# One column-tiled run per half batch for values and denominators, and head-by-head probability sums on GpSimd

## The chip, the core and the metric

One core of a Trainium2 chip runs the whole kernel. The metric is the device time of one execution in microseconds (us), median of the runs. Engines are named as in the profile: PE (TensorE matmul), PEld (its weight loads), ACT (ScalarE), DVE (VectorE), POOL (GpSimd), SP (the queue that issues most DMAs).

## The reference

Cross attention with low-rank corrections on every projection, 16 batches, 112 queries, 375 context rows, width 1024, 32 query heads on 8 key/value heads of size 32. The softmax is per query head; the output projection is added to the input.

```python
q = _lora_linear(hidden_states, Wq, Aq, Bq)   # (16, 112, 32 heads x 32)
k = _lora_linear(traces, Wk, Ak, Bk)          # (16, 375, 8 heads x 32)
v = _lora_linear(traces, Wv, Av, Bv)
scores = einsum('bhqd,bhtd->bhqt', q, k) / sqrt(32)
attn = softmax(scores, axis=-1)
context = einsum('bhqt,bhtd->bhqd', attn, v)
out = hidden_states + _lora_linear(context, Wo, Ao, Bo)
```

## The kernel before, in words

All of it runs in float32, as sums of three fast products (high and low parts). First the low-rank factors are folded into the weights and all queries are projected and written to memory (up to about 270 us of the span). Then comes a loop over the 16 batches, one step per batch of two halves; a half holds four key/value heads with four query heads each, so 448 columns per head group. After the loop the output projection runs over 14 row tiles (from about 930 us).

A step works on three batches at once, and its work is cut into pieces that `half_order` puts into one list per half. Every engine walks the same list in order and does its own share of each piece:

- **V** (values of the next batch, 3 PE matmuls of 256 columns, lines 803 to 807), **T** (transposes of the context of the batch after it; PE line 748, then ACT copies the high part, line 970, and DVE subtracts for the low part, line 1168), **K** (keys of that batch, 3 matmuls of 376 columns, lines 663 to 665). These three are the dense pieces. V is in half 0, K in half 1 (K0.k the first four heads, K1.k the second four), T in both.
- **S i**, i from 0 to 11: the scores of a head group and one of three context chunks (PE line 842, 448 columns), then `Exp` on ACT into `probs` (line 1037). S goes to bank `STB` or to bank `DEN`.
- **N i**, 0 to 15: a score matmul of the *next* batch for its row maxima (PE line 853), reduced by DVE (line 1246). N i waits until the maximum of N i-2 is taken. **M** turns the 16 maxima (PE line 858), ACT negates them (line 1044).
- **P c**, c from 0 to 2: the product of the probabilities of chunk c with the values, four matmuls that each write 32 of the 128 output columns of the array (column tiles), line 868. **D**: the denominators of the half *before*, four such matmuls on `prob_sum` with a matrix of ones (line 904), then ACT copies them (`copy_den`, line 1058) and SP stores them.
- **A**: DVE copies the attention output of the half before out of its bank (line 1228). **I, J**: DVE takes the reciprocal of the denominators, SP stores it.
- **E0 j, F0 j** and **E1 j, F1 j**: the keys leave their banks; E is two ACT copies of 32x376 (line 977), F one DVE subtraction (line 1173). E0/F0 are the first four heads, E1/F1 the second four.
- POOL adds the probabilities of the three chunks into `prob_sum` in two instructions of 1792 columns (lines 644 and 649).

The dense pieces stand in a fixed order; the others are placed by the table `PLAN` (kind, number, due time as a fraction of the half) among them, by counting the columns in `COST`. What is still in the table when the dense pieces are through is put behind them. `run_steps` says which kinds are in which step; steps 0 to 13 are full or nearly so, the last two also fold the output weights (**W**) and begin the output (**O**, **Z**). Engines and queues are in order, so a piece that waits holds all that is behind it on its engine.

## Time and profile before

| | |
|---|---|
| runs | 1071.17, 1073.62, 1074.78 us; median 1073.62 |
| span of the profiled execution | 1069.5 us (first to last instruction); the page gives no other time for it, and the median run is 4.1 us above it |
| PE busy | 997.3 us, 93% of the span |
| DVE, ACT, POOL busy | 582.0, 496.0, 286.3 us |
| granted PE clock, mean | 0.971 of full speed |
| one batch in the loop | 40.2 us (the first P of one half 0 at 512.66, of the next at 552.87) |

PE is busy nearly all the time, but a busy matmul row is not a matmul at its peak: rows overlap, so the distance from one row's start to the next one's start is what an instruction costs the engine. Idle time of DVE, ACT and POOL costs nothing unless PE waits for them.

### The profile page before, as it was taken

To read this page: it belongs to the slowest core of one execution; us is meant where nothing else is said; L and a number is where in the kernel's file an instruction comes from. 1 tells how busy PE (TensorE), PEld (TensorE's weight loads), DVE (VectorE), ACT (ScalarE), POOL (GpSimd) and SP (SyncE) were. 2 spreads that over 40 slices of the span, in tenths; PEclk is the share of its full clock that TensorE was granted. 3 is DMA by queue.
4 is the path that set the end of the run, shared out by engine and by line. 5 is a ranking of instruction groups with operands and counts; after the bars stand their busy time and mean duration, and the time that the engine had idled before them with its cause. 6 is when DMAs were issued, how large, how long until landed. Compare 5 with 4: busy or idle time off the path is not lost.

```text
span 1069.5 us, 17947 instructions
## 1 busy us (share of the span) xinstructions
PE 997.3 (93%) x5904; PEld 787.8 (74%) x5904; DVE 582.0 (54%) x1005; ACT 496.0 (46%) x971; POOL 286.3 (27%) x84
## 2 busy tenths in 40 slices
PE   6988899959999999999999999999999877999998
PEld 5878799958777777777777777777777533678886
DVE  5660213237766666666666666666666565233331
ACT  3340212234566666666666666666666544200100
POOL 1201000000344344344344344344344355300000
PEclk9999899979999999999999999999999959999999
DMA  6827342272223333333332332332331333567552
GB/s 189 233 78 200 126 149 77 78 179 76 66 94 99 68 93 96 67 93 92 71 93 91 73 93 88 75 93 87 77 93 38 84 112 84 142 206 235 183 170 78
DMA packets 104052, 118.13 MB, mean 110 GB/s; under 512 B 29152, under 2 KB 88672, under 8 KB 104016
## 3 DMA queue, kind: packets, MB, share of 16 engines
q1 hardware_dynamic: 100156, 103.99, 35.4%
q10 hardware_dynamic: 3860, 13.67, 3.5%
q8 instruction: 21, 0.34, 0.1%
q14 instruction: 15, 0.12, 0.0%
HBM read 87.59 MB, written 29.82 MB: 110 GB/s over the span
## 4 chain that ended last, share of the span: by engine, by line
PE 74%; DVE 7%; ACT 6%; DMA 6%; issue 4%; SPq 2%; ACTq 0%; POOL 0%; DVEq 0%; POOLq 0%
PE ps L663 11%; PE ps L664 11%; PE ps L665 11%; PE ps L853 9%; PE ps L868 8%; PE ps L842 7%; PE ps L748 4%; PE ps L803 3%; PE ps L805 3%; PE ps L807 3%; PE ps L904 3%; DMA ctx_in<-in_ctx_dram 2%; DMA q_scratch<-q_out_lo 2%; ACT probs L1037 2%; DMA out_dram<-residual 1%
## 5 line engine op out<-in xcount | busy, mean ns | idle before, releaser
L1246 DVE TENSOR_REDUCE maxima<-ps 112x1 f32<-112x375 f32 x512 | 271.0, 543 | 107.8 <-PE ps L853 101.1
L1037 ACT ACTIVATE probs<-ps 125x448 f32<-125x448 f32 x384 | 206.8, 543 | 132.8 <-PE ps L842 128.6
L644 POOL TENSOR_TENSOR prob_sum<-probs 125x1792 f32<-125x1792 f32 x32 | 129.2, 4039 | 391.8 <-ACT probs L1037 391.8
L853 PE MATMUL ps<-k_stack,q_stack 96*112 96x376 f32 x512 | 190.2, 372 | 7.0 <-DVE maxima L1246 5.5
L842 PE MATMUL ps<-q_stack,k_stack 97*125 97x448 f32 x384 | 147.9, 385 | 10.5 <-ACT probs L1037 10.2
L853 PEld LDWEIGHTS ps<-k_stack,q_stack 96*112 96x112 f32 x512 | 91.6, 179 | 85.8 <-DVE maxima L1246 69.0
L649 POOL TENSOR_TENSOR prob_sum<-prob_sum,probs 125x1792 f32<-125x1792 f32 x32 | 129.0, 4032 | 32.6 <-ACT probs L1037 32.5
L977 ACT ACTIVATE k_stack<-ps 32x376 fp32r<-32x376 f32 x256 | 121.4, 474 | 10.0 <-PE ps L665 6.1
L803 PE MATMUL ps<-wv_hi,ct_hi 128*125 128x256 f32 x384 | 112.6, 293 | 0.5 <-DVE k_stack L1173 0.5
L1168 DVE TENSOR_TENSOR ct_lo<-ps,ct_hi 128x375 fp32r<-128x375 f32 x128 | 70.2, 549 | 76.2 <-ACT ct_hi L970 75.6
L807 PE MATMUL ps<-wv_hi,ct_lo 128*125 128x256 f32 x384 | 108.4, 282 | 0.0
L805 PE MATMUL ps<-wv_lo,ct_hi 128*125 128x256 f32 x384 | 108.4, 282 | 0.0
L663 PE MATMUL ps<-xt_hi,wq_hi 128*128 128x448 f32 x256 | 98.7, 386 | 7.8 <-DVE q_out_lo L1162 7.1
L868 PE MATMUL ps<-probs,v 125*32 125x448 f32 x768 | 93.8, 560 | 7.6 <-ACT probs L1037 7.6
L970 ACT ACTIVATE ct_hi<-ps 128x375 fp32r<-128x375 f32 x128 | 61.9, 484 | 73.9 <-PE ps L748 71.9
L663 PE MATMUL ps<-wo_hi,attn_hi 128*128 128x512 f32 x224 | 89.9, 401 | 6.6 <-DVE attn_lo L1274 5.9
L664 PE MATMUL ps<-xt_lo,wq_hi 128*128 128x448 f32 x256 | 95.2, 372 | 0.0
L665 PE MATMUL ps<-xt_hi,wq_lo 128*128 128x448 f32 x256 | 95.0, 371 | 0.0
L1173 DVE TENSOR_TENSOR k_stack<-ps,k_stack 32x376 fp32r<-32x376 f32 x128 | 70.0, 546 | 37.7 <-ACT k_stack L977 35.0
L663 PE MATMUL ps<-ct_hi,wk_hi 128*128 128x376 f32 x256 | 89.5, 349 | 0.4 <-DVE ct_lo L1168 0.3
L664 PE MATMUL ps<-wo_lo,attn_hi 128*128 128x512 f32 x224 | 89.1, 398 | 0.0
L665 PE MATMUL ps<-wo_hi,attn_lo 128*128 128x512 f32 x224 | 89.1, 398 | 0.0
(80 smaller groups left out, 1465.4 us busy)
## 6 DMA issues: line engine op xcount, KB each, us to landing
ctx_in<-in_ctx_dram SPq DMA_DIRECT2D x16, 1500.0 KB
q_stack<-q_scratch SPq DMA_DIRECT2D x96, 224.0 KB, 4.3
x_in<-in_x_dram SPq DMA_DIRECT2D x8, 896.0 KB, 9.3
q_scratch<-q_out_hi SPq DMA_DIRECT2D x16, 448.0 KB, 2.8
q_scratch<-q_out_lo SPq DMA_DIRECT2D x16, 448.0 KB, 3.7
attn_scratch<-attn SPq DMA_DIRECT2D x32, 224.0 KB, 4.5
attn_rows<-attn_scratch SPq DMA_DIRECT2D x14, 512.0 KB, 4.9
inv_tile<-inv_scratch SPq DMA_DIRECT2D x56, 128.0 KB, 5.1
```

The source lines that it names most:

```text
L644: pool.tensor_tensor(prob_sum[:, :, :], probs[:, 0, :, :], probs[:, 1, :, :], ALU.add).then_inc(psum_added, 1)
L663: pe.matmul(dst, l_hi, r_hi, start=start, stop=False)
L664: pe.matmul(dst, l_hi, r_lo, start=False, stop=False)
L665: return pe.matmul(dst, l_lo, r_hi, start=False, stop=stop)
L803: pe.matmul(dst, ct_hi[:, k, rows], wv_hi[:, k, :], start=(k == 0 and i != 1), stop=False, skip_group_check=True)
L805: pe.matmul(dst, ct_hi[:, k, rows], wv_lo[:, k, :], start=False, stop=False, skip_group_check=True)
L807: mm = pe.matmul(dst, ct_lo[:, k, rows], wv_hi[:, k, :], start=False, stop=(k == KC - 1), skip_group_check=True)
L842: pe.matmul(ps[0:TR, score_bank(i), 0:QH], kst[cur][0:STM, g, c * TR:(c + 1) * TR], qst[cur][0:STM, g, :], start=True, stop=True).then_inc ...
L853: mm = pe.matmul(ps[0:NQ, NAT + i % 2, 0:NTE], qst[nxt][0:STK, g, rr * NQ:(rr + 1) * NQ], kst[nxt][0:STK, g, :], start=True, stop=True)
L868: mm = pe.matmul(ps[HD * j:HD * (j + 1), CTX, 0:QH], v_sb[cur][:, i, g * HD:(g + 1) * HD], probs[:, i, j, :], start=(i == 0), stop=(i == T ...
L1037: act.activation(probs[:, c, j, :], ps[0:TR, score_bank(i), 0:QH], ACT.Exp, scale=SM).then_inc(exp_done, 1)
L1246: dve.tensor_reduce(maxima[:, h, i:i + 1], ps[0:NQ, NAT + i % 2, 0:NT], AX.X, ALU.max).then_inc(max_done, 1)
```

## The change

In `PLAN` the three P pieces become one, due at 0.815 of the half, and its cost in `COST` rises from 4 to 16 times 448 columns; D has no cost any more and costs nothing on PE. Inside P, PE does the three value chunks (12 column-tiled matmuls) and at once the denominators of the *same* half (4 more). S is due every 0.065 instead of 0.07, N every 0.047 instead of 0.052, E0/F0 every 0.05 from 0.58 instead of every 0.08 from 0.62. E1/F1 move from the start of the next step's half 0 to the end of half 1, behind the last K. All odd S go to bank `DEN` and all even ones to `STB`, so S 1 now waits until ACT has copied the denominators of the half before (`den_copied`). POOL adds in eight instructions of 448 columns, one per head group, each behind its own `Exp`. SP's D waits for the earlier stores of denominators before it loads them back.

```diff
-S_IN_DEN = (3, 5, 7, 9, 11)
+S_IN_DEN = (1, 3, 5, 7, 9, 11)
 PLAN = sorted(
-    [("S", i, 0.01 + 0.07 * i) for i in range(TC * JH)]
-    + [("P", 0, 0.31), ("P", 1, 0.583), ("P", 2, 0.925), ("A", 0, 0.048), ("D", 0, 0.097)]
+    [("S", i, 0.01 + 0.065 * i) for i in range(TC * JH)]
+    + [("A", 0, 0.005), ("D", 0, 0.03), ("P", 0, 0.815)]
     + [("I", 0, 0.35), ("J", 0, 0.45)]
-    + [("N", i, 0.03 + 0.052 * i) for i in range(JH * RH)] + [("M", 0, 0.925)]
-    + [("E0", j, 0.62 + 0.08 * j) for j in range(JH)] + [("E1", j, 0.03 + 0.06 * j) for j in range(JH)]
-    + [("F0", j, 0.62 + 0.08 * j) for j in range(JH)] + [("F1", j, 0.03 + 0.06 * j) for j in range(JH)],
+    + [("N", i, 0.02 + 0.047 * i) for i in range(JH * RH)] + [("M", 0, 0.80)]
+    + [("E0", j, 0.58 + 0.05 * j) for j in range(JH)] + [("E1", j, 0.82 + 0.01 * j) for j in range(JH)]
+    + [("F0", j, 0.58 + 0.05 * j) for j in range(JH)] + [("F1", j, 0.82 + 0.01 * j) for j in range(JH)],
...
-COST = {"S": QH, "P": 4 * QH, "D": 4 * QH, "N": NTE, ...
+COST = {"S": QH, "P": 16 * QH, "N": NTE, ...
...
+        if piece[0] == "K" and piece[2] == KC - 1:
+            early = [item for item in order if item[0] in (f"E{piece[1]}", f"F{piece[1]}")]
+            order = [item for item in order if item not in early] + early
...
-                        if kind == "S" and i == 2 * JH - 1:
+                        if kind == "S" and JH <= i < 2 * JH:
+                            j = i - JH
+                            if j == 0:
+                                at_least(pool, den_done, n)
+                            pool.wait_ge(exp_done, NS * n + i + 1)
+                            pool.tensor_tensor(prob_sum[:, j, :], probs[:, 0, j, :], probs[:, 1, j, :], ALU.add
...
-                            pe.wait_ge(exp_done, NS * n + JH * (i + 1))
-                            if i == 0:
-                                at_least(pe, attn_set, n)
-                                pe.wait_ge(v_set, 2 * (b + 1))
-                            for j in range(JH):
...
-                            mm.then_inc(pv_done, 1)
-                        elif kind == "D":
-                            denominators(n - 1)
+                            pe.wait_ge(exp_done, NS * (n + 1))
+                            at_least(pe, attn_set, n)
+                            pe.wait_ge(v_set, 2 * (b + 1))
+                            for c in range(TC):
+                                for j in range(JH):
+                                    g = h * JH + j
+                                    mm = pe.matmul(ps[HD * j:HD * (j + 1), CTX, 0:QH],
+                                                   v_sb[cur][:, c, g * HD:(g + 1) * HD], probs[:, c, j, :],
+                                                   start=(c == 0), stop=(c == TC - 1))
+                                mm.then_inc(pv_done, 1)
+                            denominators(n)
...
-                            at_least(act, psum_added, 2 * n - (1 if c < 2 else 0))
+                            at_least(act, psum_added, SUMS * (n - 1) + j + 1 + (JH if c == 2 else 0))
```

With these numbers P's due time is reached only when the dense pieces are through, so P stands behind all of them. On PE, around the end of half 1 and the start of the next step (L663 to L665 keys, L868 values times probabilities, L858 maxima turned, L904 denominators, L803 to L807 next values, L842 scores), there stood before:

```order
L663 MATMUL ps<-ct_hi,wk_hi 128x376
L664 MATMUL ps<-ct_lo,wk_hi 128x376
L665 MATMUL ps<-ct_hi,wk_lo 128x376
L862 REGISTER_ALU
L868 MATMUL ps<-probs,v_81 32x448 x4
L857 REGISTER_ALU
L858 MATMUL ps<-ident,maxima 16x112
L803 MATMUL ps<-wv_hi,ct_hi 125x256
L805 MATMUL ps<-wv_lo,ct_hi 125x256
L807 MATMUL ps<-wv_hi,ct_lo 125x256
L829 REGISTER_ALU
```

and now (all lines are some ten higher: L673 to L675 keys, L878 values, L868 maxima, L913 denominators):

```order
L673 MATMUL ps<-ct_hi,wk_hi 128x376
L674 MATMUL ps<-ct_lo,wk_hi 128x376
L675 MATMUL ps<-ct_hi,wk_lo 128x376
L867 REGISTER_ALU
L868 MATMUL ps<-ident,maxima 16x112
L872 ISA
L878 MATMUL ps<-probs,v_81 32x448 x12
L911 REGISTER_ALU
L913 MATMUL ps<-prob_sum,ones 32x448 x4
L813 MATMUL ps<-wv_hi,ct_hi 125x256
```

M moved ahead of P, and the run of 16 column-tiled matmuls is the last work of the half.

On DVE, at the end of the same half (L1246 maxima, L1173 subtraction of the keys, L1228 copy of the attention output), there stood before, the loop's branch being the border of the step:

```order
L1173 TENSOR_TENSOR k_stack_78<-ps,k_stack_78 32x376
L1245 REGISTER_ALU
L1246 TENSOR_REDUCE maxima<-ps 112x1
L1245 REGISTER_ALU
L1246 TENSOR_REDUCE maxima<-ps 112x1
L1173 TENSOR_TENSOR k_stack_78<-ps,k_stack_78 32x376
L1245 REGISTER_ALU
L1246 TENSOR_REDUCE maxima<-ps 112x1
L1173 TENSOR_TENSOR k_stack_78<-ps,k_stack_78 32x376
```

and now (L1254 maxima, L1181 keys, L1236 attention copy):

```order
L1181 TENSOR_TENSOR k_stack_79<-ps,k_stack_79 32x376
L1253 REGISTER_ALU
L1254 TENSOR_REDUCE maxima<-ps 112x1
L1253 REGISTER_ALU
L1254 TENSOR_REDUCE maxima<-ps 112x1
L1181 TENSOR_TENSOR k_stack_79<-ps,k_stack_79 32x376
L1253 REGISTER_ALU
L1254 TENSOR_REDUCE maxima<-ps 112x1
L1181 TENSOR_TENSOR k_stack_79<-ps,k_stack_79 32x376 x5
L1234 REGISTER_ALU
L1236 COPY attn_66<-ps 128x448
```

The order of the first subtractions and maxima is the same; the four subtractions of the second heads now stand right behind the fourth one, ahead of the attention copy.

On ACT the same end of half 1 is, with the change (L1045 exponentials, L985 key copies, L1052 negated maxima, L1066 copied denominators; the branch is the border of the step):

```order
L1045 ACTIVATE probs<-ps 125x448
L985 ACTIVATE k_stack_78<-ps 32x376 x2
L1052 ACTIVATE neg_max<-ps 16x112
L982 REGISTER_ALU
L131 REGISTER_ALU
L985 ACTIVATE k_stack_78<-ps 32x376 x8
L394 REGISTER_ALU
L394 COMPARE_AND_BRANCH
L1045 ACTIVATE probs<-ps 125x448
L1066 ACTIVATE denominators<-ps 128x448
L1045 ACTIVATE probs<-ps 125x448 x5
```

The eight key copies stand in one block ahead of the next step's first exponential, and the copy of the denominators behind that exponential.

## Rows read from the trace of the kernel before

**Rows 1.** The page: busy time by engine; granted PE clock in 40 slices, in tenths.

```profile
PE 997.3 (93%) x5904; PEld 787.8 (74%) x5904; DVE 582.0 (54%) x1005; ACT 496.0 (46%) x971; POOL 286.3 (27%) x84
...
PEclk9999899979999999999999999999999959999999
```

**Rows 2.** Timeline of PE, 510 to 531 us: start, duration, line, operation, [idle before <-releaser].

```profile
511.22 0.36 PE L842 MATMUL ps<-q_stack,k_stack 97*125 97x448 f32 x1
511.69 0.43 PE L853 MATMUL ps<-k_stack,q_stack 96*112 96x376 f32 x1
512.66 0.96 PE L868 MATMUL ps<-probs,v 125*32 125x448 f32 x8 [0.54 <-ACT probs L1037]
...
517.60 0.36 PE L842 MATMUL ps<-q_stack,k_stack 97*125 97x448 f32 x1
517.89 0.96 PE L868 MATMUL ps<-probs,v 125*32 125x448 f32 x8
518.78 0.42 PE L853 MATMUL ps<-k_stack,q_stack 96*112 96x376 f32 x1
519.04 0.48 PE L748 MATMUL ps<-ident,ctx_in 125*128 125x125 f32 x3
...
525.61 0.48 PE L748 MATMUL ps<-ident,ctx_in 125*128 125x125 f32 x3
...
526.66 0.34 PE L853 MATMUL ps<-k_stack,q_stack 96*112 96x376 f32 x1
527.26 0.54 PE L748 MATMUL ps<-ident,ctx_in 125*128 125x125 f32 x3 [0.26 <-DVE ct_lo L1168]
```

**Rows 3.** Line 868 from 517.5 to 519: ns min/median/max, first and last start.

```profile
L868 PEld LDWEIGHTS ps<-probs,v x8: 105/108/109, 517.9 to 517.9; 125*32 125x32 f32 x8
L868 PE MATMUL ps<-probs,v x8: 538/551/564, 517.9 to 518.3; 125*32 125x448 f32 x8
```

**Rows 4.** Timeline of PE, 530 to 553 us.

```profile
539.06 0.34 PE L663 MATMUL ps<-ct_hi,wk_hi 128*128 128x376 f32 x1
...
539.58 0.33 PE L663 MATMUL ps<-ct_hi,wk_hi 128*128 128x376 f32 x1
...
540.10 0.34 PE L853 MATMUL ps<-k_stack,q_stack 96*112 96x376 f32 x1
540.28 0.37 PE L842 MATMUL ps<-q_stack,k_stack 97*125 97x448 f32 x1
540.49 0.33 PE L663 MATMUL ps<-ct_hi,wk_hi 128*128 128x376 f32 x1
```

**Rows 5.** Timeline of ACT, 536 to 553 us.

```profile
539.09 0.54 ACT L1037 ACTIVATE probs<-ps 125x448 f32<-125x448 f32 x1
539.66 0.96 ACT L977 ACTIVATE k_stack<-ps 32x376 fp32r<-32x376 f32 x2
540.69 0.54 ACT L1037 ACTIVATE probs<-ps 125x448 f32<-125x448 f32 x1
...
542.15 1.96 ACT L977 ACTIVATE k_stack<-ps 32x376 fp32r<-32x376 f32 x4
```

**Rows 6.** Timeline of DVE, 536 to 553 us.

```profile
539.46 0.54 DVE L1173 TENSOR_TENSOR k_stack<-ps,k_stack 32x376 fp32r<-32x376 f32 x1
540.03 0.55 DVE L1246 TENSOR_REDUCE maxima<-ps 112x1 f32<-112x375 f32 x1
540.65 0.54 DVE L1173 TENSOR_TENSOR k_stack<-ps,k_stack 32x376 fp32r<-32x376 f32 x1
```

**Rows 7.** Groups by line: busy us, mean ns of one | idle before.

```profile
L644 POOL TENSOR_TENSOR prob_sum<-probs 125x1792 f32<-125x1792 f32 x32 | 129.2, 4039 | 391.8 <-ACT probs L1037 391.8
...
L1058 ACT ACTIVATE denominators<-ps 128x448 f32<-128x448 f32 x32 | 17.4, 543 | 17.4 <-PE ps L904 17.1
```

**Rows 8.** Timeline of PE, 843 to 932 us.

```profile
850.56 0.74 PE L842 MATMUL ps<-q_stack,k_stack 97*125 97x448 f32 x1 [2.46 <-ACT probs L1037]
...
877.18 0.80 PE L663 MATMUL ps<-wo_hi,attn_hi 128*128 128x512 f32 x1 [3.68 <-DVE attn_lo L1274]
```

More of the change, by code:

```diff
@@ L42 @@
 NS = TC * JH
+SUMS = 2 * JH
 NN = JH * RH
@@ L112, in half_order @@
         at += COST[piece[0]]
+        if piece[0] == "K" and piece[2] == KC - 1:
+            early = [item for item in order if item[0] in (f"E{piece[1]}", f"F{piece[1]}")]
+            order = [item for item in order if item not in early] + early
     order += [(kind, i, 0) for kind, i, _ in plan]
-    assert "K" not in has or order.index(("K", 0, KC - 1)) < order.index(("E0", 0, 0))
+    for half in range(HALVES if "K" in has else 0):
+        assert order.index(("K", half, KC - 1)) < order.index((f"E{half}", 0, 0))
     return order + [("E", 0, 0)]
@@ L382, in run_steps @@
         def run_steps(eng, step, wo_factors):
-            full = ({"A", "D", "V", "T", "N", "Q", "E1"}, {"A", "D", "G", "T", "K", "C", "N", "Q"})
+            full = ({"A", "D", "V", "T", "N", "Q"}, {"A", "D", "G", "T", "K", "C", "N", "Q"})
             step(-1, 0, (set(), {"K"}))
-            step(-1, 1, ({"V", "T", "N", "E1"}, {"T", "K", "C", "N"}))
+            step(-1, 1, ({"V", "T", "N"}, {"T", "K", "C", "N"}))
             wo_factors()
@@ L391, in run_steps @@
             step(B // 2 - 2, 1, (full[0], full[1] - {"C"}))
-            step(B // 2 - 1, 0, ({"A", "D", "V", "N", "E1"}, {"A", "D", "G", "N", "W0"}))
+            step(B // 2 - 1, 0, ({"A", "D", "V", "N"}, {"A", "D", "G", "N", "W0"}))
             step(B // 2 - 1, 1, ({"A", "D", "W1"}, {"A", "D", "G", "W2"}))
@@ L567, in step @@
                         elif kind == "D":
+                            if "G" in has[h]:
+                                at_least(sp, den_stored, 16 * 2 * b)
                             store_den(sp, 2 * b + h - 1, b - 1 + h, 1 - h)
@@ L640, in step @@
                     for kind, i, k in half_order(h, has[h]):
[L641 to L649 removed]
+                        if kind == "S" and JH <= i < 2 * JH:
[4 more added lines that the diff above has]
+                            pool.tensor_tensor(prob_sum[:, j, :], probs[:, 0, j, :], probs[:, 1, j, :], ALU.add
+                                               ).then_inc(psum_added, 1)
+                        elif kind == "S" and i >= 2 * JH:
+                            j = i - 2 * JH
+                            pool.wait_ge(psum_added, SUMS * n + j + 1)
+                            pool.wait_ge(exp_done, NS * n + i + 1)
+                            pool.tensor_tensor(prob_sum[:, j, :], prob_sum[:, j, :], probs[:, 2, j, :], ALU.add
                                                ).then_inc(psum_added, 1)
@@ L900, in denominators @@
             def denominators(n):
-                pe.wait_ge(psum_added, 2 * n + 2)
+                pe.wait_ge(psum_added, SUMS * (n + 1))
                 for j in range(JH):
@@ L911, in _ @@
             run_steps(pe, step, wo_factors)
-            denominators(2 * B - 1)
             def tile(pair, par):
@@ L1029, in step @@
                         elif kind == "E1":
[L1030 removed]
+                            k_hi(b + 2, cur, 1, i)
                         elif kind == "S":
```

18 lines of the change are left out of this document (3 added, 15 removed).

## The prediction, made before the changed kernel ran

> **What bounds the kernel now.** I read the page first: PE is busy for 93% of the span and the granted clock is full in nearly every slice [rows 1], so a time is gained where PE's issue gets shorter or a wait of PE goes, and lost where PE waits anew. Then the timeline of PE inside one batch of the loop. Two things are to be seen there.
>
> First, a column-tiled run costs more than its streaming. A score matmul is followed by the next row after 0.21 us (540.28 to 540.49) [rows 4], but by P after 0.29 (517.60 to 517.89) [rows 2]; P takes 0.89 to the next row (517.89 to 518.78); and the row behind it takes 0.26 (518.78 to 519.04) where such a row takes 0.18 (540.10 to 540.28) [rows 4]. One run of four matmuls so costs 0.89 + 0.08 + 0.08 = 1.05 us. Inside it there are eight records in two passes of four, the second starting about 0.40 behind the first: 0.96 for all eight less 0.54 for the last, less the 0.02 by which the four of a pass are staggered [rows 2, 3]. The second pass needs no more than 0.40 either, so the rest of the 0.89 is 0.09 of emptying.
>
> Second, PE waits at three places of each batch, two in half 0 and one as half 1 begins: N 3 comes 0.47 behind S instead of 0.21 (511.22 to 511.69), the first P 0.97 behind N instead of 0.26 (511.69 to 512.66, for ACT's exponential), and T 5 comes 0.60 behind N instead of 0.18 (526.66 to 527.26, for DVE's low part) [rows 2]. That is 0.26 + 0.71 + 0.42 = 1.4 us of the 40.2 that a batch takes; without waits it would take 38.8.
>
> **The change, part by part, per batch.**
>
> *Merging.* Four runs per half become one of eight passes: 7 x 0.40 + 0.49 + 0.16 = 3.45 instead of 4 x 1.05 = 4.20, so 0.75 to 0.8 per half, **-1.6 us** per batch with the four entries and exits unrounded. No row shows two groups back to back. If nothing is gained between groups except the three entries and exits, it is 3 x 0.17 = 0.5 per half (-1.0); if passes follow each other without their 0.03 of slack, 0.95 per half (-1.9). I take 0.40, since a pass behind a pass is what the trace has. The trace shows all eight weight loads starting at 517.9, 0.4 us before the second pass that uses four of them [rows 3]. The Trainium skill ("TensorE: Matmul & The Clock Gate", Part 3, on what overlaps) says that a weight load overlaps matmuls in flight only if it is for other row groups; all of these use the same 125 rows, so by that rule each pass would show its load and merging would give only the entries and exits, -1.0 a batch, and the time of the third rival below. The trace here speaks against it.
>
> *Old waits.* P now stands behind all S, T 5 is separated from T 4 by the run, and half 0 has no E1/F1 in its ACT and DVE queues: **-1.4**.
>
> *New wait at S 1.* The odd banks are now shared with the denominators, and ACT copies these behind the first exponential, since it stands behind it in its queue. In half 1 the run's end is zero; K0.0 takes 0.52 + 0.09, so S 0 is issued at 0.6, its exponential starts 0.40 later (0.37 of matmul and 0.03), the copy follows some 0.5 behind and takes 0.54 [rows 4, 7]: done at 2.0. S 1 has only N 0, T 5 and N 1 ahead of it (0.18 + 0.33 + 0.25, T with its longer successor) and could go at 1.5. Wait 0.55. In half 0 ACT first finishes the eight copies of E1: they begin some 0.5 behind the start of the run and take 4 x 0.98 (1.96 for four) [rows 5], so they end about 1.2 us behind its end; exponential and copy end at 2.3, S 1 could go at 1.7. Wait 0.65. Together **+1.2**.
>
> *New wait at the end of half 1.* This is the largest. The order is S 8, N 11, K, first pair, N 12, S 9, K, second pair, N 13, K, S 10, N 14, third pair, K, N 15, S 11, fourth pair, K, K, M, P (with "pair" for the two E0 copies of one head and its F0). ACT can do an exponential and a pair every 1.60 us (539.09 to 540.69) [rows 5], and on DVE each F0 stands ahead of the next maximum: F starts 0.03 behind its pair (539.66 + 0.96 to 540.65), the maximum 0.57 behind F [rows 5, 6]. With the exponential of S 8 at zero, F 0 starts at 1.6, the maximum of N 12 ends at 2.7, that of N 13 at 4.3, that of N 15 at 6.0. PE, at 0.18 for N, 0.21 for S and 0.52 for K [rows 4], would be at N 14 at 2.3, and must wait for N 12's maximum: 0.4. It would then be at N 15 at 3.4, and waits for N 13's to 4.3: 0.9. It is at M at 5.75 and waits for N 15's to 6.0: 0.2. **+1.5.** Before, the same pairs stood 0.08 of a half apart, with more K between, and PE did not wait: K, K, N, S follow without a gap [rows 4].
>
> *New wait at the end of half 0.* N 15 now stands behind T 3 on DVE. A T needs 1.6 us from issue to the end of its low part (525.61 to 527.26, less 0.05) [rows 2], and the maximum behind it ends at 2.2; M is only 1.8 behind T 3. **+0.45.** The same chain delays N 12 and N 14 (behind T 1 and T 2) by 0.2 to 0.25 each, **+0.5**. In half 1, T 7's low part and then the reciprocal stand ahead of the maxima for N 8 and N 10: about **+0.6**.
>
> *E1/F1* then run beside the 3.3 us of the merged run, the fourth pair's tail excepted (counted at S 1). *POOL's* eight adds cost about 4039/4 = 1.0 us each [rows 7]; the last begins when the last exponential ends, before the run starts, and the denominators come 6 x 0.40 = 2.4 us into it: nothing. *SP's* extra wait is for a store of the half before: nothing. The DMAs of M, of the context and of the queries are needed half a step later or more: nothing, unless the half shrinks by several us.
>
> Sum per batch: -1.6 - 1.4 + 1.2 + 1.5 + 0.45 + 0.5 + 0.6 = **+1.2 us**. The single waits are good to 0.1 or 0.2 each, the sum to 0.8. Steps 0 to 13 make 14 x 1.2 = **+17**.
>
> *Ends.* In the last four halves merging gains about 1 us each, since some of it is at the low clock: -4. PE waits there 3.68 for the first tile of the output (877.18) [rows 8], because the fourth fold stood last in its half; it now stands in the middle: -3. In the step before the loop, four F1 in a row stand ahead of the first maxima: +2. Together **-5**, and the folds moved among the maxima could make it 0 or -12.
>
> So the profiled execution would have 1069.5 + 17 - 5 = 1081.5 of span; the median run lies 4.1 above the span, hence **1085.5 us**, 1.1% slower.
>
> **Rivals.**
>
> *Faster.* The new waits don't add up: where S 1 has waited, ACT and DVE are ahead, and less is left for the later places. The point from which it decides is their sum: below 3.0 us per batch (merging and the old waits) the change gains. If the end of half 1 and the T chains cost nothing, and only S 1 stays, a batch gains 1.8, 14 x 1.8 = 25, with the ends 1044 us. For it: nothing in the list except P forbids PE to run dense, and DVE and ACT are busy only 54 and 46%. Against: those are averages, and in the stretch of the pairs ACT is full [rows 5]. 0.20.
>
> *A wash.* New waits of 3.0 to 3.5 instead of 4.25: within 3 us of before, which is about what a measurement of this kernel can tell from no change (0.3%). 0.12.
>
> *The run doesn't merge,* each group empties the array before the next as it did alone. Then -1.0 instead of -1.6 per batch, 14 x 0.6 = 8 more: 1094. For it: no row of two groups in sequence. Against: the loads that start early [rows 3]. 0.10.
>
> *The clock.* It fell to 1.2 GHz in one slice late in the kernel [rows 1], where PE had idle gaps of 2.46 and 3.68 us [rows 8]. If the new waits let it fall in the loop, the merged run alone would cost 3.3 us more in a half: some 45 us in all over half of the halves, 1130. Against: none of the new waits is over 1 us, and the loop held 2.4 GHz with waits of 0.7. 0.03.
>
> **How the numbers follow.** The forecast has 0.55; with the two slower rivals slower has 0.68, same 0.12, faster 0.20. The forecast's own range is 14 x (0.4 to 2.0) with the ends at 0 to -12: 1073 to 1101. To hold 8 in 10 the range takes in the wash and the nearer part of the faster case and leaves out its far part and the clock: 1060 to 1101.
>
> **What would show it.** Right: P and D as one group of 32 records lasting 3.3 to 3.5 us; a batch of 41 to 42 us; PE waits for `maxima` and, at the second score matmul of each half, for the copied denominators; no wait of P for an exponential of more than 0.1. Wrong in the merging if the group takes 3.6 or more; wrong in the waits if a batch is under 40 us, or if the waits for `maxima` in the last 5 us of half 1 sum to under 0.7.

## The result, and the profile after

The changed kernel takes **1092.73 us** (median of 4 runs, 1091.31 to 1096.95) against 1072.55 (median of 4 runs): ratio 1.0203, 95% interval 1.0173 to 1.0233. It is 2% slower. Of all executions behind the times here and below one is left out of its ratio: 1351.61 us of a later kernel, at a mean granted clock of 0.655.

| | before | after |
|---|---|---|
| span of the profiled execution | 1069.5 us | 1090.4 us |
| first half step of the loop, step 0 | 21.20 us | 29.17 us |
| half 0 / half 1, mean of steps 1 to 13 | 21.03 / 19.17 us | 20.77 / 20.56 us |
| one batch | 40.20 us | 41.33 us |
| from the first S of step 14 to the last PE row | 238.3 us | 236.0 us |

A half is counted from the start of its S 0 on PE to the next half's S 0. The 20.9 us of span are: step 0 with +9.0 (half 0 +8.0, half 1 +1.0), 13 steps of +1.13 = +14.7, the rest of the kernel -2.3, and -0.45 at the loop's start.

From the page of after, the two lines that answer to [rows 1]:

```profile
PE 990.9 (91%) x5904; PEld 807.6 (74%) x5904; DVE 579.8 (53%) x1005; ACT 489.8 (45%) x971; POOL 320.6 (29%) x276
...
PEclk9999999989999999999999999999999957989999
```

PE is busy 6 us less in a span that is 21 us longer: the merging took work off PE, and new waits took more than that back.

The timeline of PE in one batch of the loop (half 1 ends with the run at 516.03), against [rows 2, 4]:

```profile
500.64 0.47 PE L852 MATMUL ps<-q_stack,k_stack 97*125 97x448 f32 x1 [0.57 <-ACT denominators L1066]
...
507.01 0.43 PE L863 MATMUL ps<-k_stack,q_stack 96*112 96x376 f32 x1 [0.28 <-DVE maxima L1254]
507.27 0.38 PE L852 MATMUL ps<-q_stack,k_stack 97*125 97x448 f32 x1
...
512.67 0.43 PE L863 MATMUL ps<-k_stack,q_stack 96*112 96x376 f32 x1 [0.22 <-DVE maxima L1254]
512.93 0.34 PE L673 MATMUL ps<-ct_hi,wk_hi 128*128 128x376 f32 x1
...
514.23 0.42 PE L863 MATMUL ps<-k_stack,q_stack 96*112 96x376 f32 x1 [0.61 <-DVE maxima L1254]
514.49 0.37 PE L852 MATMUL ps<-q_stack,k_stack 97*125 97x448 f32 x1
...
515.84 0.26 PE L868 MATMUL ps<-ident,maxima 112*16 112x112 f32 x1
516.03 2.46 PE L878 MATMUL ps<-probs,v 125*32 125x448 f32 x24
518.31 0.94 PE L913 MATMUL ps<-prob_sum,ones 125*32 125x448 f32 x8
519.18 0.38 PE L813 MATMUL ps<-wv_hi,ct_hi 128*125 128x256 f32 x1
...
521.65 0.47 PE L852 MATMUL ps<-q_stack,k_stack 97*125 97x448 f32 x1 [0.59 <-ACT denominators L1066]
```

The run is one group of 32 records, 3.15 us from 516.03 to 519.18. Around it PE waits at S 1 of both halves for the copied denominators and at N 8, N 14 and N 15 of half 1 for maxima; half 0, which follows, has two more, at N 14 (0.48 behind its predecessor, where 0.20 is usual) and at M (0.44, where 0.12 is usual):

```profile
532.84 0.36 PE L852 MATMUL ps<-q_stack,k_stack 97*125 97x448 f32 x1
533.32 0.43 PE L863 MATMUL ps<-k_stack,q_stack 96*112 96x376 f32 x1
...
536.05 0.26 PE L868 MATMUL ps<-ident,maxima 112*16 112x112 f32 x1 [0.16 <-DVE maxima L1254]
```

The idle time in brackets understates a wait: by distances between starts, N 15 comes 0.95 behind its predecessor where 0.17 is usual. The view of waits sums them up:

```profile
PE ps L863 <- DVE maxima L1254: 28.1, 46, 7.7
...
PE ps L852 <- ACT denominators L1066: 20.3, 30, 2.7
```

What they wait for is seen on the other two engines in the same stretch. ACT, against [rows 5], does the eight E1 copies, then the exponential of S 0, then the denominators, which end as S 1 of half 0 starts:

```profile
516.69 3.91 ACT L985 ACTIVATE k_stack<-ps 32x376 fp32r<-32x376 f32 x8
520.62 0.54 ACT L1045 ACTIVATE probs<-ps 125x448 f32<-125x448 f32 x1
521.06 0.54 ACT L1066 ACTIVATE denominators<-ps 128x448 f32<-128x448 f32 x1
```

DVE, against [rows 6], does each F0 ahead of the maximum that PE needs:

```profile
513.05 0.54 DVE L1181 TENSOR_TENSOR k_stack<-ps,k_stack 32x376 fp32r<-32x376 f32 x1 [0.43 <-ACT k_stack L985]
513.62 1.00 DVE L1254 TENSOR_REDUCE maxima<-ps 112x1 f32<-112x375 f32 x2
514.66 0.55 DVE L1181 TENSOR_TENSOR k_stack<-ps,k_stack 32x376 fp32r<-32x376 f32 x1
```

At the two ends of the loop two places stand out. In step 0, PE has the longest idle time of steps 0 to 13, and its clock falls: the granted clock from 271 to 277 us is 0.50, the 1.2 GHz level, where the kernel before has 1.00 from 268 to 280 us.

```profile
271.34 0.74 PE L852 MATMUL ps<-q_stack,k_stack 97*125 97x448 f32 x1 [6.36 <-DVE a_stack_o L1131]
```

```profile
core 0: us, PE busy (x) PEld busy (x) DVE busy (x) ACT busy (x) POOL busy (x), PEclk, DMA share, GB/s
271.00:277.00 6.00, 5.66 (x23) 5.50 (x24) 2.39 (x5) 1.40 (x3) 0.00 (x0) 0.50 0.01 3
```

DVE of the changed kernel there, and of the kernel before:

```profile
266.50 0.55 DVE L1181 TENSOR_TENSOR k_stack<-ps,k_stack 32x376 fp32r<-32x376 f32 x1 [0.44 <-ACT k_stack L985]
267.58 2.45 DVE L1126 TENSOR_TENSOR b_stack_o<-b_in,b_stack_o 32x1024 fp32r<-32x1024 f32 x2 [0.53 <-ACT b_stack_o L951]
270.06 1.23 DVE L1131 SCALAR_TENSOR_TENSOR a_stack_o<-ps,a_stack_o 64x1024 fp32r<-64x1024 f32 x1
```

```profile
263.70 2.45 DVE L1118 TENSOR_TENSOR b_stack_o<-b_in,b_stack_o 32x1024 fp32r<-32x1024 f32 x2 [1.22 <-ACT b_stack_o L943]
266.18 1.23 DVE L1123 SCALAR_TENSOR_TENSOR a_stack_o<-ps,a_stack_o 64x1024 fp32r<-64x1024 f32 x1
```

The factor's low part comes 3.9 us later, behind the F1 block of the step before, and S 1 is now the first score in the bank that the factor's transposes used.

In step 14, half 1 takes 32.0 us instead of 25.4, with a new wait of PE of 7.73 us for maxima at 889.76; on DVE the normalising and splitting of the first output tile stand ahead of these:

```profile
889.76 0.66 PE L863 MATMUL ps<-k_stack,q_stack 96*112 96x376 f32 x1 [7.73 <-DVE maxima L1254]
```

```profile
883.55 3.35 DVE L1277 TENSOR_TENSOR attn_rows<-attn_rows,inv_tile 128x1024 f32<-128x1024 f32 x1
888.03 1.22 DVE L1282 TENSOR_TENSOR attn_lo<-attn_rows,attn_hi 128x1024 fp32r<-128x1024 f32 x1 [1.12 <-ACT attn_hi L1072]
889.17 0.99 DVE L1254 TENSOR_REDUCE maxima<-ps 112x1 f32<-112x375 f32 x2
```

### The profile page after: what moved, and what is told of

Its sections match the earlier page's. It is cut to its first block and busy times, and to the rows that moved or that the text cites. A ratio compares the mean times of both kernels' runs of the same rounds, so it can differ in the third digit from the quotient of the medians.

```text
span 1090.4 us, 18568 instructions
## 1 busy us (share of the span) xinstructions
PE 990.9 (91%) x5904; PEld 807.6 (74%) x5904; DVE 579.8 (53%) x1005; ACT 489.8 (45%) x971; POOL 320.6 (29%) x276
## 5 line engine op out<-in xcount | busy, mean ns | idle before, releaser
L1045 ACT ACTIVATE probs<-ps 125x448 f32<-125x448 f32 x384 | 208.0, 544 | 233.4 <-PE ps L852 232.1
L1254 DVE TENSOR_REDUCE maxima<-ps 112x1 f32<-112x375 f32 x512 | 268.0, 542 | 71.3 <-PE ps L863 65.0
L653 POOL TENSOR_TENSOR prob_sum<-probs 125x448 f32<-125x448 f32 x128 | 146.1, 1160 | 372.5 <-ACT probs L1045 372.4
L659 POOL TENSOR_TENSOR prob_sum<-prob_sum,probs 125x448 f32<-125x448 f32 x128 | 148.0, 1163 | 36.7 <-ACT probs L1045 33.1
L985 ACT ACTIVATE k_stack<-ps 32x376 fp32r<-32x376 f32 x256 | 121.3, 474 | 12.2 <-PE ps L675 8.4
L673 PE MATMUL ps<-xt_hi,wq_hi 128*128 128x448 f32 x256 | 98.5, 385 | 7.8 <-DVE q_out_lo L1170 7.0
L1181 DVE TENSOR_TENSOR k_stack<-ps,k_stack 32x376 fp32r<-32x376 f32 x128 | 69.9, 546 | 66.4 <-ACT k_stack L985 65.9
L852 PEld LDWEIGHTS ps<-q_stack,k_stack 97*125 97x125 f32 x384 | 73.8, 192 | 40.4 <-ACT denominators L1066 28.4
L675 PE MATMUL ps<-xt_hi,wq_lo 128*128 128x448 f32 x256 | 94.7, 370 | 0.0
L673 PE MATMUL ps<-wo_hi,attn_hi 128*128 128x512 f32 x224 | 89.7, 401 | 3.4 <-DVE attn_lo L1282 3.4
L673 PE MATMUL ps<-ct_hi,wk_hi 128*128 128x376 f32 x256 | 88.8, 347 | 0.3 <-DVE ct_lo L1176 0.3
L675 PE MATMUL ps<-wo_hi,attn_lo 128*128 128x512 f32 x224 | 89.1, 398 | 0.0
L878 PE MATMUL ps<-probs,v 125*32 125x448 f32 x768 | 83.1, 568 | 3.2 <-ACT probs L1045 3.2
```

The source lines that it names most:

```text
L653: pool.tensor_tensor(prob_sum[:, j, :], probs[:, 0, j, :], probs[:, 1, j, :], ALU.add).then_inc(psum_added, 1)
L659: pool.tensor_tensor(prob_sum[:, j, :], prob_sum[:, j, :], probs[:, 2, j, :], ALU.add).then_inc(psum_added, 1)
L673: pe.matmul(dst, l_hi, r_hi, start=start, stop=False)
L675: return pe.matmul(dst, l_lo, r_hi, start=False, stop=stop)
L852: pe.matmul(ps[0:TR, score_bank(i), 0:QH], kst[cur][0:STM, g, c * TR:(c + 1) * TR], qst[cur][0:STM, g, :], start=True, stop=True).then_inc ...
L985: op = act.activation(kst[par][HD * quad:HD * (quad + 1), half * JH + j, :], ps[HD * j:HD * (j + 1), (VA, TURN)[half], 0:NTE], ACT.Copy)
```

## The experiments

Theory: the merging gains what was worked out, and the loss is the places that the new list gives to small pieces of ACT and DVE work. Rivals: each wait, once removed, comes back at the next place (the engines are full there); the GpSimd part costs or gains by itself; the run gains nothing. Times of different groups of runs are compared by their ratio to the kernel before, which ran beside each of them. The edits are shown shortened to the entries that change; the first four start from the changed kernel, and the second of them turned out to hold two edits.

**S 1 in the other bank.**

```diff
-S_IN_DEN = (1, 3, 5, 7, 9, 11)
+S_IN_DEN = (3, 5, 7, 9, 11)
```

> The changed kernel with S 1 back in the bank of the even scores, so that neither the copied denominators nor, in step 0, the low part of the output factors stands ahead of S 1 (S 3 has these waits again). Theory A (the loss is made of new PE waits, the merged run is a gain of about 1.8 us a batch): the waits at S 1 (0.73 and 0.65 us a batch in the changed kernel) shrink to 0.1 to 0.3 each, a batch falls from 41.35 to about 40.3, and the first half of step 0 from 29.2 to about 21.5 us; in all 20 to 24 us faster than the changed kernel. Theory B (the waits only move: a wait taken away at S 1 comes back at N 8 and at the key copies, because ACT and DVE idle during the merged run and lack that time): the first half of step 0 gains its 7 us, a batch stays within 0.3 of 41.35.

Measured: 1092.47 us, ratio 1.0194 (1.0159 to 1.0230); a batch 41.12, as Theory B had it, and the first half step 27.96, where both theories had about 22. The wait for the denominators is gone, but in half 0, S 1 waits for the late exponential and N 2 for a late maximum:

```profile
522.21 0.47 PE L852 MATMUL ps<-q_stack,k_stack 97*125 97x448 f32 x1 [0.18 <-ACT probs L1045]
523.34 0.42 PE L863 MATMUL ps<-k_stack,q_stack 96*112 96x376 f32 x1 [0.31 <-DVE maxima L1254]
```

By distances between starts the 0.73 us at S 1 of half 1 and 0.76 at S 1 of half 0 became 0.30 and 0.34, plus 0.13 at N 3 of half 1 and 0.47 at N 2 of half 0. So the bank is a small part of the cause, 0.21 us of a batch: ACT and DVE are late as a half begins, and the bank mostly decides which piece notices.

**Maxima ahead of F0, and M behind the run.**

```diff
-("M", 0, 0.80)
+("M", 0, 0.82)
-("F0", j, 0.58 + 0.05 * j)
+("F0", j, 0.655 + 0.05 * j)
```

> The changed kernel with F0 due 0.075 of the half later, so that the last maxima of half 1 stand ahead of the key subtractions on DVE, and with M behind the merged run. Theory A: the waits of N 14 and N 15 (0.38 and 0.78) and of M (0.1 to 0.2 in each half) go, the run then waits about 0.3 for the last exponential, and ACT ends the copies of E1 up to 0.5 later, which S 1 of half 0 feels; a batch falls from 41.35 to about 40.3, 12 to 16 us in all. Theory B (ACT's pace of 1.6 us per exponential and pair of key copies is what holds the end of half 1, not the place of F0): the run waits for the last exponential instead, and a batch stays within 0.3.

Measured: 1141.69 us, ratio 1.0649 (1.0608 to 1.0690). Half 1 fell from 20.56 to 19.72 us, half 0 rose from 20.77 to 24.69. Neither theory had this. With M behind the run, ACT's negation waits for the run's end, and so do the eight E1 copies behind it, which the run had covered; S 1 waits for all of them:

```profile
535.70 0.25 ACT L1052 ACTIVATE neg_max<-ps 16x112 fp32r<-16x112 f32 x1 [2.51 <-PE ps L868]
535.86 3.92 ACT L985 ACTIVATE k_stack<-ps 32x376 fp32r<-32x376 f32 x8
...
540.84 0.56 PE L852 MATMUL ps<-q_stack,k_stack 97*125 97x448 f32 x1 [3.34 <-ACT denominators L1066]
```

Not all of the loss is waiting. Behind this wait PE's granted clock is 0.52 from 541 to 543.5 us, about its 1.2 GHz level (1.00 from 520 to 536), and so it is in every step. S 1 comes 2.75 us later than in the changed kernel, and the rows from there to S 3 take 1.4 us more.

The edit was two edits in one, so the later F0 was repeated alone (below).

**GpSimd's two additions per half put back** (1792 columns each, as before; all else as changed).

```diff
-    pool.tensor_tensor(prob_sum[:, j, :], probs[:, 0, j, :], probs[:, 1, j, :], ALU.add
+    pool.tensor_tensor(prob_sum[:, :, :], probs[:, 0, :, :], probs[:, 1, :, :], ALU.add
...
-    pool.tensor_tensor(prob_sum[:, j, :], prob_sum[:, j, :], probs[:, 2, j, :], ALU.add
+    pool.tensor_tensor(prob_sum[:, :, :], prob_sum[:, :, :], probs[:, 2, :, :], ALU.add
```

> The changed kernel with the two additions of 1792 columns on POOL per half, as before the change. Theory A: the last addition of about 4.0 us begins after the last exponential and ends about 1 us after PE has done the value chunks, so the denominators wait about 0.9 in half 0 and 1.0 in half 1; 41.35 becomes about 43.2, 25 us slower than the changed kernel. Theory C (the eight additions of 1.16 us, 0.16 longer than a quarter of the old ones, are what slows the loop): faster than the changed kernel by 5 us or more.

Measured: 1122.6 us, ratio 1.0480 (1.0442 to 1.0518); a batch 43.39. The denominators at the end of the run now wait for the last sum:

```profile
511.58 0.96 PE L910 MATMUL ps<-prob_sum,ones 125*32 125x448 f32 x8 [0.97 <-POOL prob_sum L656]
```

So the head-by-head sums are what lets the denominators join the run. That they cost nothing by themselves is read from the changed kernel: in its view of waits PE and ACT never wait for a sum, and PEld once, 1.3 us at 925.46, in step 15.

**The run broken up** (chunk 0 behind S 11, chunks 1 and 2 each behind a following dense piece, the denominators, X, where the run was).

```diff
+    order[at] = ("X", 0, 0)
+    order.insert(first + 1, ("P", 0, 0))
...
+            order.insert(at + 1, ("P", c, 0))
```

> The changed kernel with the merged run broken up: value chunk 0 right behind S 11, chunks 1 and 2 behind the next dense pieces, the denominators where the run was; nothing else moves. Theory A: each half pays four runs of 1.05 again instead of one of 3.14 and its entry and exit, 0.85 to 0.9 a half; the small wait of M (0.1 to 0.2) hides in it; a batch 42.7 to 43.0, 20 to 24 us slower than the changed kernel. Theory D (merging gives only entries and exits, the emptying between groups was hidden): 0.5 a half, 42.3, 14 us. Theory B (work inside the end of the half gives ACT and DVE time): within 5 us.

Measured: 1155.08 us, ratio 1.0795 (1.0746 to 1.0844). None of the three theories had that time. Half 1 went from 20.56 to 21.32 us, +0.76; with M's wait of 0.11 gone that is 0.87 for three more groups, as Theory A had it, and not the 0.5 of Theory D. Half 0 went to 23.85: M now stands behind chunk 2, ACT's negation waits 2.66 us for it, the E1 copies behind that lost the long run that covered them, and S 1 waits 2.50 us. Of the steps 1 to 13, seven have a half 0 of 23.2 us; the other six have 24.6, and there the granted clock falls behind that wait (0.53 from 588.66 to 591.66 us). In the seven, 2.4 us more are 1.9 at S 1, less the 0.32 of M, which leaves 0.8 for the groups, close to half 1. And the run is also the cover of the E1 block.

**F0 later, alone** (the F0 line of the second edit, M left where it was).

```diff
-("F0", j, 0.58 + 0.05 * j)
+("F0", j, 0.655 + 0.05 * j)
```

> Only the GpSimd-fed low-half copies on VectorE (the F0 group) are moved later in each half, from a due time of 0.58 + 0.05 j to 0.655 + 0.05 j, so that the row maxima of the last scores stand ahead of them on VectorE; the maximum that closes the batch stays where it was. Theory A (each wait of the score matmuls for maxima, 0.43 + 0.39 + 0.77 us in half 1 of the changed kernel, is a matter of what stands ahead on VectorE): half 1 falls from 20.56 to 19.7 us, half 0 stays at 20.8 to 21.2, a batch takes 40.5 instead of 41.3, the kernel is 10 to 13 us faster than the change. Theory B (a wait removed comes back at the next place, as it did when the bank of the denominators was changed): a batch takes 41.1 to 41.4 us and the time stays within 3 us of the change.

F0 is not fed by GpSimd, as the expectation says, but by ACT's copies. Measured: 1088.62 us, ratio 1.0142 (1.0110 to 1.0173), between the theories; half 1 19.72, half 0 21.25, a batch 40.96. Of the waits of scores for maxima in half 1 only N 8 is left, and more than half of the gain comes back in half 0: the run now begins earlier, waiting 0.27 us for the last exponential, and at the same ACT pace the E1 copies reach further into half 0.

```profile
515.11 2.46 PE L878 MATMUL ps<-probs,v 125*32 125x448 f32 x24 [0.27 <-ACT probs L1045]
...
521.20 0.47 PE L852 MATMUL ps<-q_stack,k_stack 97*125 97x448 f32 x1 [1.05 <-ACT denominators L1066]
```

**Denominators ahead of the first exponential, attention copy later.**

```diff
-("A", 0, 0.005), ("D", 0, 0.03)
+("A", 0, 0.06), ("D", 0, 0.005)
```

> Only the heads of two queues change in each half: ScalarE copies the denominators out of PSUM ahead of the first exponential (due 0.005 instead of 0.03), and VectorE copies the attention tile behind the first score maximum (due 0.06 instead of 0.005). Theory A (the first score matmuls of a half wait 0.75 to 0.80 us for the copy of the denominators because one exponential stands ahead of it): these waits fall to 0.1 to 0.2 us in both halves, a batch takes 40.1 to 40.5 us instead of 41.3, the kernel is 11 to 16 us faster than the change. Theory B (the exponential that now stands behind the copy is itself late, and the wait moves to the transposes or to the maxima): a batch stays within 0.3 us of 41.3.

Measured: 1083.61 us, ratio 1.0114 (1.0083 to 1.0146); a batch 40.65. S 1 of half 1 no longer waits, S 1 of half 0 by 0.32 instead of 0.75. In half 1, N 3 now waits 0.62 (0.47 of it idle), since the attention copy stands ahead of a maximum:

```profile
500.01 0.43 PE L863 MATMUL ps<-k_stack,q_stack 96*112 96x376 f32 x1 [0.47 <-DVE maxima L1254]
```

Both theories are half right: of 1.5 us at S 1, 0.7 stayed away.

**The places together** (the order of the sixth edit at the head; E0 and F0 spaced by hand; the output factor ahead of the first fold; normalising and splitting beside the run, the last two as shown further below).

```diff
-("A", 0, 0.005), ("D", 0, 0.03)
+("A", 0, 0.06), ("D", 0, 0.005)
-("E0", j, 0.58 + 0.05 * j)
+("E0", j, (0.52, 0.58, 0.64, 0.73)[j])
-("F0", j, 0.58 + 0.05 * j)
+("F0", j, (0.60, 0.655, 0.71, 0.755)[j])
```

> The merged run is kept and the queues around it are put in the order of who is waited for: denominators ahead of the first exponential, the attention tile behind the first maximum, the low-half copies and additions of both engines spaced so that the last maxima come first, the output factor ahead of the first step's folds, and the normalising and splitting of the first two output tiles placed beside the merged run instead of ahead of maxima. Theory A (the waits of the changed kernel are queue order and go away together): a batch takes 38.5 to 39.3 us (40.2 before, 41.3 with the change), the first half step 21 to 23 us instead of 29.2, and the kernel 1045 to 1058 us, faster than both. Theory B (the copies of the fold and the maxima fill VectorE and ScalarE at the end of a half, so that a wait is only moved): a batch takes 40.5 to 41.3 us, and the time is 1070 to 1085 us, from the first step and the tail alone.

Measured: 1064.27 us, ratio 0.9926 (0.9906 to 0.9946); a batch 39.79, the first half step 24.5. Between the theories. By distances, six waits were left in a batch: 0.31 at S 1, 0.28 at N 14 and 0.32 at M in half 0, 0.62 at N 3, 0.43 at N 8 and 0.53 at M in half 1. The next list of places went by four of them and left out the two at M, of which the longer one is:

```profile
504.06 0.26 PE L868 MATMUL ps<-ident,maxima 112*16 112x112 f32 x1 [0.39 <-DVE maxima L1252]
```

**The two places at the ends of the loop, one at a time** (each in the changed kernel).

```diff
-            step(-1, 1, ({"V", "T", "N"}, {"T", "K", "C", "N"}))
             wo_factors()
+            step(-1, 1, ({"V", "T", "N"}, {"T", "K", "C", "N"}))
```

> The changed kernel with one move outside the loop: the block that makes the low-rank output factors stands ahead of the first K fold step instead of behind it, on every engine, as the copies of that step now end in a block. Theory A (the first score matmul in the denominator bank waits 6.4 us because VectorE and ScalarE do the eight plus eight copies of that step ahead of the factor's low part): the first half step falls from 29.2 us to 21 to 25 us, all later half steps stay as they are, and the kernel is 4 to 8 us faster than the change (1085 to 1089 us). Theory B (the factor's work is late by its own inputs, so that the wait moves to maxima or copies): the first half step stays above 27 us, the time within 2 us of the change.

Measured: 1089.26 us, ratio 1.0173 (1.0141 to 1.0205). The first half step falls from 29.17 to 24.53 us. With S 1 in the other bank (the first experiment) it had stayed at 27.96, as exponentials and maxima are late there too (PE waits 4.11 and 1.47 us for them). The next kernel, whose first step is that of the change, has 27.87 with the same wait of 6.36: single executions differ by 1.3 us there, so the 4.6 is good to about that. What is left of its excess is the F1 block ahead of the first maxima:

```profile
271.67 0.43 PE L863 MATMUL ps<-k_stack,q_stack 96*112 96x376 f32 x1 [3.02 <-DVE maxima L1254]
```

The other place, with DVE's part of the edit (ACT's split moves in the same way):

```diff
-                            if i == OLAG - 1:
-                                normalise(0, 0)
-                                split(0, 0)
-                        elif kind == "O" and i == 3:
-                            normalise(0, 1)
-                            split(0, 1)
+                        elif kind == "P" and ("W0" in has[h] or "W1" in has[h]):
+                            normalise(0, int("W1" in has[h]))
+                            split(0, int("W1" in has[h]))
```

> The changed kernel with one move in the last two steps: normalising and splitting the first two output tiles stands beside the merged run at the end of a half, on VectorE and ScalarE, instead of ahead of the maxima. Theory A (the 7.7 us wait of the scores for maxima in the first step of the tail is the normalising and splitting that stand ahead of them on VectorE): half 14.1 falls from 32.0 us to 25 to 28 us, half 15.0 stays at 27 to 29 us, and the kernel is 4 to 7 us faster than the change. Theory B (the output projection then waits for the split in the next half): 14.1 falls but 15.0 grows by as much, and the time stays within 2 us.

Measured: 1089.27 us, ratio 1.0186 (1.0154 to 1.0218). Half 14.1 falls from 32.02 to 27.41 us, 15.0 goes from 27.72 to 28.45; the longest wait for maxima there is 2.10 instead of 7.73 us. For both edits the place is shown by the trace; that the whole is faster is not, since both intervals overlap that of the change.

**A second round of places** (N 6 and N 12 go ahead of the transpose next to them, the first E1 ahead of M; A, D, E0 and F0 move once more; shown against the kernel with the places together).

```diff
-("A", 0, 0.06), ("D", 0, 0.005)
+("A", 0, 0.12), ("D", 0, 0.0)
-("N", i, 0.02 + 0.047 * i)
+("N", i, {6: 0.268, 12: 0.568, 14: 0.69}.get(i, 0.02 + 0.047 * i))
-("E0", j, (0.52, 0.58, 0.64, 0.73)[j]), ("E1", j, 0.82 + 0.01 * j)
+("E0", j, 0.47 + 0.07 * j), ("E1", j, (0.79, 0.82, 0.83, 0.84)[j])
-("F0", j, (0.60, 0.655, 0.71, 0.755)[j])
+("F0", j, (0.56, 0.62, 0.69, 0.775)[j])
```

> The version with all queues in the order of who is waited for, in which four waits were left in a batch (0.31 us of the first denominator-bank score in half 0, 0.28 us of a score in half 0 for maxima; 0.62 and 0.43 us in half 1), with these places moved: the attention copy behind the third maximum, the copies of the denominators at the head of the half, scores 6 and 12 of the maxima ahead of the transpose next to them, the first fold's copies earlier and the last of them behind the last maximum, one copy of the second fold ahead of the run. Theory A (these waits, too, are places in a queue): a batch takes 38.0 to 38.9 us instead of 39.8, and the kernel 1040 to 1054 us. Theory B (VectorE and ScalarE are near full at the pace of 1.25 to 1.6 us a score, so that a wait is only moved): a batch takes 39.4 to 40.0 us, the time 1060 to 1067 us.

Measured: **1055.82 us**, ratio 0.9859 (0.9832 to 0.9886); batches of 39.2 us but for one. Faster than both kernels, between the theories again. What is left is, above all, the run of half 1, which waits for the last exponential, and in half 0 M, which waits for the last maximum:

```profile
502.52 2.46 PE L879 MATMUL ps<-probs,v 125*32 125x448 f32 x24 [0.54 <-ACT probs L1046]
...
521.53 0.26 PE L869 MATMUL ps<-ident,maxima 112*16 112x112 f32 x1 [0.16 <-DVE maxima L1253]
```

**The run of half 0 split in that kernel.** The order of the end of half 0, before and after the edit:

```diff
-S11 V1.7 V2.7 M T4 P(chunks 0, 1, 2 and denominators)
+S11 P(chunk 0) V1.7 M P(chunk 1) V2.7 P(chunk 2) T4 P(denominators)
```

> The spaced version, with the merged run of half 0 alone split into its four groups of four matmuls, and the last dense pieces of the half, which stood ahead of the run, between the groups (V, M behind the first, V behind the second, a transpose behind the third). Half 1 keeps its merged run. Theory A (an isolated group costs 1.05 us with entry, emptying and exit, the merged run 3.14 + 0.18 = 3.3 us): half 0 grows from 19.73 by 0.8 to 0.9 us to 20.5 to 20.7, half 1 stays at 19.4, the ratio to the kernel before rises by 0.010 to 0.013, from 0.986 to 0.996 to 0.999. Theory B (merging is worth little, the gain of the spaced version is all from queue order): half 0 stays within 0.3 us.

Measured: 1062.79 us, ratio 0.9917 (0.9890 to 0.9944); half 0 20.30 instead of 19.73, half 1 unchanged at 19.43. The expected 0.8 to 0.9 are there, less a wait: M now has a group between it and N 15 and doesn't wait (0.12 behind its predecessor instead of 0.45), so 0.57 + 0.33 = 0.90 us is the price of the three splits.

```profile
485.03 0.96 PE L895 MATMUL ps<-probs,v 125*32 125x448 f32 x8
485.92 0.38 PE L818 MATMUL ps<-wv_hi,ct_hi 128*125 128x256 f32 x1
...
486.38 0.26 PE L873 MATMUL ps<-ident,maxima 112*16 112x112 f32 x1
486.57 0.96 PE L895 MATMUL ps<-probs,v 125*32 125x448 f32 x8
```

It also divides the gain of the spaced version in half 0: from 21.03 us before to 20.30 with the run split, by order alone, and to 19.73 with the run merged. Half 1 has no such gain: 19.43 us with its run merged, against 19.17 before. The order costs more there than the 0.88 that merging gives.

**Three last places** (N 8 due at 0.36 instead of 0.396 and the reciprocal behind it; the last low parts of the output weight on VectorE instead of GpSimd, of which the choice is shown).

```diff
-("I", 0, 0.35), ("J", 0, 0.45)
+("I", 0, 0.37), ("J", 0, 0.46)
...
-    return int(g % 2 == 1 and not KC <= g < QKV_BLOCKS)
+    return int(g % 2 == 1 and not KC <= g < QKV_BLOCKS and g < QKV_BLOCKS + 4)
```

> The spaced version with three more places: score 8 of the maxima one piece earlier and the reciprocal behind it; the low parts of the last output-weight blocks on VectorE instead of GpSimd, where one of 3.2 us stood ahead of the sums of the last half. Theory A (these are places in a queue as well): half 0 falls from 19.73 to 19.5, a batch from 39.2 to 38.9, the wait of 4.4 us for the sums in step 15 shrinks to under 1.5 us, the kernel is 4 to 8 us faster than the spaced version (ratio 0.979 to 0.982). Theory B (moved again): ratio 0.984 to 0.988.

Measured: 1052.38 us, ratio 0.9811 (0.9787 to 0.9834), the fastest of the kernels run. But half 0 stays at 19.73, and the wait for the sums in step 15 falls only from 4.37 to 2.05 us; the span of its profiled execution, the slowest of six, is 1053.8 us against 1053.7 for the spaced version, and the two intervals just touch. That these three places gain anything is not shown.

## Why the prediction was right

It said 1085.5 us, 1.1% slower, and a range of 1060 to 1101; measured were 1092.73 and 2.0%. The sign and the mechanism of the loop held, and two terms at its ends were mis-sized in the same direction. The number is better than the working: by span it was 1081.5 against 1090.4, 8.9 off. The 4.1 us that it added for the median, from one profiled execution, was 1.8 when the changed kernel was profiled (1092.24 with a span of 1090.4), and that hides a part of it. The low end of its own range was also added up wrong: 14 x 0.4 with ends of -12 is 1067, not 1073; the stated range takes that in.

**The loop.** Forecast +1.2 us a batch, measured +1.13. By its terms, in us:

| term of the sum | forecast | measured |
|---|---|---|
| merging | -1.6 | -1.76 |
| old waits (N 5, P, T 5) gone | -1.4 | -1.4 |
| S 1, half 1 / half 0 | 0.55 / 0.65 | 0.73 / 0.76 |
| end of half 1: N 14, N 15, M | 0.4, 0.9, 0.2 | 0.39, 0.77, 0.1 |
| M at the end of half 0 | 0.45 | 0.32 |
| N 12 and N 14, half 0 | 0.5 | 0.28 |
| N 8 and N 10, half 1 | 0.6 | 0.43 |

The score at 511.69 that the prediction calls N 3 is N 5 by the list. At N 12 of half 0 and N 10 of half 1 there was no wait; what was measured is at N 14 and N 8 alone.

*Merging* gained a little more than taken: passes follow each other after 0.376 us on average (0.400 the first time), not 0.40, and the run takes 3.14 from its start to the next row, where 7 x 0.40 + 0.49 = 3.29 was forecast (the group of 32 records itself lasts 3.22, a little under the 3.3 to 3.5 named as its sign). With 0.18 for entry and exit, 4.20 per half became 3.32. The split run confirms the size by itself (0.90 us for three more groups).

*The waits* sum to 3.80 instead of 4.25; the largest, at N 15, stands where the forecast put it, for the reason it gave. Left out was that the row behind a waiting row costs more too: 0.26 from N 14 to the next row (512.67 to 512.93), where 0.18 is usual. At some four places more than before that makes 0.4 us, and so the sum is right partly by luck, because small errors cancel: 40.20 - 1.76 - 1.4 + 3.80 + 0.4 = 41.24, against 41.33 measured.

**Step 0** is where it was most wrong. "In the step before the loop, four F1 in a row stand ahead of the first maxima: +2" named the block, and the maxima do wait for it: with the factor moved away, a wait of 3.02 us and 24.53 instead of 21.2 remain. What it missed is that the output factor's low part stands behind that block on DVE too, and that S 1, whose bank was changed, is the first to need it. That wait is 6.36 us, and the clock it let fall makes the rows behind it slower; together the first step is +9.0 instead of +3.2 (the +2 and the +1.2 of every step). Moving the factor took 4.6 us of it away.

**The other ends.** Forecast -7 together (-4 merging, -3 fold position), measured -2.3 from step 14 on. The first tile's wait of 3.68 [rows 8] did go, but normalising moved ahead of maxima in half 14.1, a wait of 7.73. How much of the -2.3 is the change is not shown: the kernel with the factor first has the same work from step 1 on, and from the first S of step 14 it took 239.0 us where the change took 236.0. Either way the -7 is missed, and "the folds moved among the maxima could make it 0" was the right bound.

**Rivals.** The time alone would have spoken for the wrong one: 1092.73 lies nearer to the 1094 of the rival in which the run doesn't merge than to 1085.5. By the rows that rival is ruled out. The Trainium skill ("TensorE: Matmul & The Clock Gate", Part 3) has weight loads overlap matmuls in flight only for other row groups. Here four loads for the third pass, on the same 125 rows, start as the second pass does, 0.38 us ahead of their own, and every pass follows on time:

```profile
516.03 0.16 PEld L878 LDWEIGHTS ps<-probs,v 125*32 125x32 f32 x8
516.43 0.13 PEld L878 LDWEIGHTS ps<-probs,v 125*32 125x32 f32 x4 [0.24 <-issue]
516.81 0.13 PEld L878 LDWEIGHTS ps<-probs,v 125*32 125x32 f32 x4 [0.24 <-issue]
```

The trace speaks against the rule. The faster rival gave as its point of decision new waits under 3.0 us a batch. The change has 3.80; the version with the places together has 2.5 at its six places and is faster than before, which bears the rival's reasoning out, though in another kernel. The clock fell in step 0 and, as before [rows 1], late in the kernel, but not in the steps between (granted 1.00 from 300 to 850 us). What the rival of the clock feared did happen in two of the kernels above, with idle times of 2.50 and 3.34 us in a step.

**Still open:** some 0.1 us of a batch is not assigned, and what the last three places gained, if anything. E1/F1 were never put back at the start of half 0 alone, so what that part of the change gives or takes by itself isn't measured. How far the order could still be improved wasn't tried: in the spaced version PE waits at M and, in half 1, for the last exponential.

## What to carry to other kernels

When a transfer of PE work into one long block frees PE time, list what each in-order queue does around the block: the block is cover for the work that stands beside it and a cliff for what stands behind it, and the gain is only kept if the pieces that PE waits for come first in those queues. Remove such waits together, not singly: alone, a wait of 1.5 us at S 1 gave back 0.2 to 0.7 us, while many of them, with the two places at the ends of the loop, in two rounds turned 2.0% slower into 1.4% faster. Look also at the first and the last steps, where a moved piece passes other work (here a factor that nobody had needed early before).

## What was not expected of the hardware

- Column-tiled groups of four, issued back to back, follow each other after 0.376 us per pass of 448 columns, and into another accumulation bank (values to denominators) at the same pace.
- The row behind a matmul that has waited comes 0.08 to 0.11 us later: 0.26 us behind a score for maxima that waited, as behind a column-tiled group, where 0.17 to 0.18 is usual.
- GpSimd's addition of 448 columns takes 1.16 us, where a quarter of its 1792-column addition [rows 7] is 1.01; eight a half cost 9.3 us of GpSimd's time instead of 8.1, which nobody waits for in the loop:

```profile
L653 POOL TENSOR_TENSOR prob_sum<-probs 125x448 f32<-125x448 f32 x128 | 146.1, 1160 | 372.5 <-ACT probs L1045 372.4
```

- After the new wait of 6.36 us the clock stood at its 1.2 GHz level (granted 0.50 from 271 to 277 us); in the steps behind, with waits of up to 0.8 us, it held 2.4 GHz (mean grant 1.00 from 300 to 850 us). With an idle time of 3.34 us at S 1 of half 0 (M behind the run) it fell in every step, with one of 2.50 us (the run broken up) in six of the steps 1 to 13. The page's 40 slices hide this: those of the kernel with M behind the run show 9 in all these steps.
